# A recurrent attention block and a 64-expert feed-forward block on one core: three late shared tiles in place of four, a one-tile last batch, and the final wait on SyncE

## What is computed

```
x = x + attn(layernorm(x))       # r, k, v projections, a decayed running sum, a norm over the
                                 # whole sequence, an output projection
x = x + ffn(layernorm(x))
# ffn, E=64 experts of 512x384 (gate, up) and 384x512 (down), each token takes its best K=4:
logits = xf @ w_router.T ;  top_vals, top_idx = top_k(logits, 4) ;  w = softmax(top_vals)
per expert e, up to 64 tokens:  y = (silu(x_e @ w_gate[e]) * (x_e @ w_up[e])) @ w_down[e]
combined[token] += y * w
combined += (silu(xf @ w_sh_gate) * (xf @ w_sh_up)) @ w_sh_down     # shared expert, all 2048 tokens
```

## Time and profile before

| | us |
|---|---|
| median of 3 runs | 703.15 |
| lowest and highest | 702.74, 703.49 |
| span of the profiled execution, first to last instruction | 700.6 |
| PE busy | 666.0 (95%) |
| DVE busy | 324.1 (46%) |
| POOL busy | 218.7 (31%) |
| ACT busy | 162.1 (23%) |

### The profile page before, as it was taken

How to read it: one execution, slowest core, us unless ns; L and a number is a source line. 1 busy time by engine, 2 the same in 40 slices (tenths; PEclk the granted TensorE clock), 3 DMA queues, 4 the chain that set the end, 5 groups by cost and what they waited for, 6 DMA issues and landing times. The chain is left out here.

```text
span 700.6 us, 8995 instructions
## 1 busy us (share of the span) xinstructions
PE 666.0 (95%) x3229; PEld 402.0 (57%) x3229; DVE 324.1 (46%) x779; ACT 162.1 (23%) x267; POOL 218.7 (31%) x209
## 2 busy tenths in 40 slices
PE   4999999999999999999999999999999999999982
PEld 3687878888878754444455455455445554554430
DVE  6887567759868771332332233222323323232321
ACT  5922215633111411121211111111112112111210
POOL 5537446435648131022222102221221212212012
PEclk9999999999999999999999999999999999999997
DMA  8201006713784987599999999999999999999983
GB/s 321 77 27 35 1 31 201 265 60 123 269 313 192 354 307 271 210 376 387 388 405 404 385 369 389 399 391 404 370 387 388 402 372 384 387 403 395 362 322 43
DMA packets 52347, 202.65 MB, mean 289 GB/s; under 512 B 7340, under 2 KB 7468, under 8 KB 51920
## 3 DMA queue, kind: packets, MB, share of 16 engines
q1 hardware_dynamic: 36512, 169.23, 60.9%
q0 software_dynamic: 8928, 21.31, 12.7%
q10 hardware_dynamic: 6864, 11.54, 4.4%
HBM read 178.66 MB, written 23.59 MB: 289 GB/s over the span
## 5 line engine op out<-in xcount | busy, mean ns | idle before, releaser
L630 POOL DMA_INDIRECT out_dram<-ym,midx x32 | 51.3, 1602 | 297.1 <-DVE ym L1235 119.5
L1590 PE MATMUL bank<-w_sb,xT 128*64 128x384 f32 x768 | 129.1, 489 | 0.8 <-ACT xT L857 0.8
L1369 PE MATMUL bank<-x_hi,w_parts 128*128 128x512 f32 x368 | 115.0, 395 | 2.5 <-DVE x_lo L970 2.2
L1611 PE MATMUL bank<-w_sb,guT 128*64 128x512 f32 x384 | 88.0, 593 | 2.5 <-DMA w_sb<-in_L_ffn_w_down 2.0
L1590 PEld LDWEIGHTS bank<-w_sb,xT 128*64 128x64 f32 x768 | 53.0, 137 | 63.8 <-issue 60.1
L1369 PEld LDWEIGHTS bank<-x_hi,w_parts 128*128 128x128 f32 x368 | 69.7, 190 | 18.2 <-DVE x_lo L970 3.0
L1369 PE MATMUL bank<-x_lo,w_parts 128*128 128x512 f32 x184 | 71.0, 395 | 0.0
L1174 DVE TENSOR_TENSOR gu<-sg,bank 128x384 f32<-128x384 f32 x32 | 17.7, 554 | 114.3 <-issue 107.4
L1502 PE MATMUL bank<-sh_sb,xS 128*128 128x384 f32 x192 | 63.9, 486 | 0.0
L1611 PEld LDWEIGHTS bank<-w_sb,guT 128*64 128x64 f32 x384 | 27.6, 137 | 50.6 <-issue 50.5
L1502 PEld LDWEIGHTS bank<-sh_sb,xS 128*128 128x128 f32 x192 | 35.7, 191 | 22.3
(11 more groups left out here) (189 smaller groups left out, 949.3 us busy)
## 6 DMA issues: line engine op xcount, KB each, us to landing
w_sb<-in_L_ffn_w_down SPq DMA_DIRECT2D x64, 768.0 KB
w_sb<-in_L_ffn_w_gate SPq DMA_DIRECT2D x48, 768.0 KB, 19.2
w_sb<-in_L_ffn_w_up SPq DMA_DIRECT2D x48, 768.0 KB
extra<-in_L_ffn_w_gate SPq DMA_DIRECT2D x16, 768.0 KB
extra<-in_L_ffn_w_up SPq DMA_DIRECT2D x16, 768.0 KB
ring<-in_L_attn_x SPq DMA_DIRECT2D x14, 256.0 KB, 3.5
xt_dram<-xwT ACTq DMA_DIRECT2D x12, 256.0 KB, 2.8
xS<-xt_dram SPq DMA_DIRECT2D x12, 256.0 KB, 17.2
```

What stands on the lines that cost most here:

```text
L630: pool.indirect_dma_start(out=out[:, :], out_offset=bass.IndirectOffsetOnAxis(ap=midx[j % 3][u][:, :], axis=0), in_=ym[u][:, :], in_offset ...
L1369: ins = pe.matmul(ps[u][:, :], w, xp, start=(n == 0), stop=(n == len(parts) - 1))
L1590: ins = pe.matmul(ps[e * C:(e + 1) * C, 0:I], xT[:, c, e * C:(e + 1) * C], gate_up(2 * j + u, e, k)[:, c, :], start=(c == 0), stop=(c == K ...
L1611: ins = pe.matmul(pair_bank(j, u)[e * C:(e + 1) * C, :], guT[0][:, c, e * C:(e + 1) * C], down(2 * j + u, e)[:, c, :], start=(c == 0), sto ...
```

## The change

- `LEAD` goes from 4 to 3: tiles 13, 14 and 15 are late, and tile 12 becomes ordinary. Its residual and its transpose are now stored by ACT ahead of the groups, its transpose is read back by SP, and its result goes through `yS` and a batch.
- `FIRST` goes from 2 to 1: the 13 ordinary tiles are worked in groups 1 to 13. Group 0 has no shared tile of its own (it still finishes the third late one), nor have groups 14 and 15.
- The batches of three go out in groups 3, 6, 9 and 12, and one of one tile in group 13.
- SP no longer waits for `u_ready[2]` ahead of the up matrices of pair 3.
- The wait for the last add moves from the end of POOL's program to the end of SP's.

The places in memory that hang on `LATE` (the start of `extra`) move by one tile with it.

```diff
--- before.py
+++ after.py
@@ -51,11 +51,11 @@
 PIECES = 1
 FILL = 2 * PIECES * 16
 ADD = 16
-LEAD = 4
+LEAD = 3
 TAIL = 3
 SHARED = TOKENS // P - LEAD
 LATE = TOKENS // P - LEAD
-FIRST = 2
+FIRST = 1
 
 
 def moe_block(nc, x, wr, wk, wv, wo, decay, gn_w, gn_b, w_router, w_gate, w_up, w_down,
@@ -229,11 +229,11 @@
 
         def has_shared(j):
 
-            return j == 0 or FIRST <= j < FIRST + SHARED
+            return FIRST <= j < FIRST + SHARED
 
         def item(j):
 
-            return LEAD + j - FIRST if j else TAIL
+            return LEAD + j - FIRST
 
         def in_parts(j, u):
 
@@ -260,7 +260,11 @@
 
             return ap.rearrange("p (m c) -> p c m", c=n)[:, c, :]
 
-        BATCHES = range(FIRST + 2, FIRST + SHARED, 3)
+        BATCHES = [*range(FIRST + 2, FIRST + SHARED, 3), FIRST + SHARED - 1]
+
+        def batch(j):
+            last = j - FIRST
+            return last // 3 * 3, last + 1
 
         def landed(j, u):
 
@@ -469,7 +473,6 @@
                 sp.wait_ge(x2_stored[i], turned_stores(i))
                 sp.wait_ge(xw_stored[i], 16 * SEQS * TILES // 4)
             fill_matrix(sp, 3, 0)
-            sp.wait_ge(u_ready[2], 1)
             fill_matrix(sp, 3, 1, (1,))
             sp.wait_ge(tok_turned, 1)
             fill_matrix(sp, 3, 1, (0,))
@@ -482,6 +485,7 @@
                     load_matrix(p, k)
             load_down(2 * GROUPS - 2)
             load_down(2 * GROUPS - 1)
+            sp.wait_ge(added, landed(GROUPS - 1, 1))
 
 
         @block.gpsimd
@@ -640,8 +644,9 @@
                     pool.wait_ge(yS_ready, j - FIRST + 1 + LEAD)
                     pool.wait_ge(added, landed(j, 0))
                     pool.nop(nofuse=True)
-                    pool.dma_start(out[(j - FIRST - 2) * P:(j - FIRST + 1) * P, :].rearrange("(a p) m -> p a m", p=P),
-                                   yS[:, :, :], accum_op=ALU.add).then_inc(added, ADD)
+                    t0, t1 = batch(j)
+                    pool.dma_start(out[t0 * P:t1 * P, :].rearrange("(a p) m -> p a m", p=P),
+                                   yS[:, 0:t1 - t0, :], accum_op=ALU.add).then_inc(added, ADD)
                 add_pair(j, 1, landed(j - 1, 1) if j == GROUPS - 1 else landed(j, 0) + ADD * (j in BATCHES))
 
             for i in range(4):
@@ -662,7 +667,6 @@
                 if j == 0:
                     pool.wait_ge(late_stored, 16 * LEAD)
                 add_group(j)
-            pool.wait_ge(added, landed(GROUPS - 1, 1))
 
 
         @block.scalar
@@ -898,9 +902,7 @@
                     turned_tokens(j + 1, 0)
                 else:
                     pair_out(j, 1)
-                if first:
-                    store_late(TAIL)
-                elif shared:
+                if shared:
                     shared_out(j - FIRST)
 
             def shared_turn_copy(t):
@@ -1292,8 +1294,6 @@
                 else:
                     turn_copy(j, 1)
                 merged_out(j, 0)
-                if first:
-                    shared_residual(TAIL)
                 same_tokens(j, 1)
 
             for j in range(GROUPS):
@@ -1621,8 +1621,6 @@
                 turn_tokens(j, 1)
                 if first:
                     down_shared(TAIL - 1)
-                    for w in range(2):
-                        late_product(TAIL, w)
                 elif shared:
                     for w in range(2):
                         shared_product(j - FIRST, w)
```

## The result

| | before | changed |
|---|---|---|
| median of 20 runs, us | 702.75 | 704.67 |
| lowest and highest | 702.05, 703.53 | 701.48, 706.10 |
| ratio, 95% interval | | 1.0023 (1.0016 to 1.003) |
| profiled execution, its own time | not shown | 704.01 |
| its span | 700.6 | 702.2 |

The forecast was 699.6 us with a range of 696.8 to 703.4, and the median lies above the range. The two spans differ by 1.6 us, the medians by 1.9. The sum had a change of -3.5, so 5.1 us of the span have to be accounted for.

The account below looks back on a forecast made before the run. Groups bound by PE while weights arrive in time, otherwise by DMA; the end by the chain of adds and POOL's drain. -0.5 - 1.0 + 0.4 + 0.9 - 3.3 = -3.5 us from 703.15 gives 699.6 us, range 696.8 to 703.4.

Parts of the forecast that it names:

- Step 1: Shared tile moved from group 0 to group 1: group 2 starts at 311.40 against 311.87, -0.5 us.
- Step 2: Weights land 3.4 us sooner at the end, so an add there meets less traffic: -1.0 us (0 to -1.5).
- Step 3: Chain of adds to `out`, group 12 to group 13: 54.2 us against 53.8, +0.4 us (-3.7 to +1.6).
- the rival of the one-tile batch: Group 13's one-tile batch costs as much as three tiles, link 15.8 us instead of 9.4: 706.0 us; chance 0.05.
- Step 4: Ahead of the groups, SP's loads slide towards the first gather and delay it: +0.9 us (0 to 3.3).
- Step 5: Last wait moved to SP at the program's end, POOL's drain runs beside the last add's landing: -3.3 us (bound 0).
- the first rival: At the program's end, POOL's drain waits for the adds, 3.4 us from the landing on: 703.0 us; chance 0.12.
- the two rivals: At the end, POOL's drain waits for the adds, 703.0 us (0.12); ahead of the groups, gather delayed 3.3 us, 702.0 (0.09).
- The signs of being wrong: POOL's drain ending over 3 us after landing; group 13's second add over 2 us off 668 + 0.9; groups after 265 us.

Follow-up runs that it names:

- The filler: Changed kernel with three products that nobody reads added on PE ahead of its wait for the first gathered tokens; 702.71 us, ratio to before 0.9999.

## Why the prediction was wrong

- **Step 1** (-0.5): right, -0.48.
- **Step 2** (-1.0): the mechanism was right. PE's wait of 1.99 us on the weights is gone, and in its place PE waits as long for the adds, as the step said: L1611 at 679.98 us stands behind 1.86 us of waiting for DVE's copy to `ym`. The add issued at 679.95 takes 4.70 us where it took 6.00, 1.3 less. The net up to the last add is -0.4, since the last adds wait for DVE's copies and not only for the add before, inside the bounds of 0 to -1.5.
- **Step 3** (+0.4): right. From the first add of group 12 to the second of group 13 it is 670.67 - 616.57 = 54.1 us (forecast 54.2), and the one-tile link is 670.67 - 660.79 = 9.9 (forecast 9.4). The rule of the Trainium skill, "DMA: Bandwidth & Descriptors", section "Anatomy of one DMA", by which three tiles and one differ by 1.2 us, does not hold for these adds under full DMA, where the two differ by 5.6 us: the links take 9.9, 12.1 and 15.5 us for one, two and three tiles (the last 641.51 - 625.99). So the rival of the one-tile batch, the one that would have made it slower, was false.
- **Step 4** (+0.9): failed by its size, +2.9 measured. The gather's delay, for which the step had bounds of 0 to 3.3, was 1.2, near what I took. What the sum lacked was the second effect: a wait of 2 us makes the product behind it run at the lower clock, which costs 1.7 us more (7.07 against 5.38). The sum put it at nothing, without a word on it. The filler shows that this part comes with PE's idleness. The trace before could not price it at this place, but it had a wait of 0.8 us there, and any delay was going to lengthen just that wait. The delay of SP's load was read as "a few us"; it was 5.9, and the first 2.4 of such a delay cost nothing.
- **Step 5** (-3.3): failed, -0.7 in the trace, and 0.8 and 0.6 us by the medians of two pairs of runs, the second inside the spread. The step took POOL's drain for a fixed time that could run while the add was landing. Its other bound, 0, and the first rival (0.12) were nearly right: the drain waits for the landing. I had set against that rival that the drain took 3.4 us although all had landed. The run with work ahead of the drain shows that this spoke for neither: the time is paid even 5.6 us after the landing, and can't be paid before it. The section "The DRAIN you can't avoid" in the Trainium skill's "VectorE: DVE Perf Modes" gives its 12 ns for the drains that the runtime puts ahead of a kernel and behind it. The drains of this program's own end (L66) take 7 ns on SP after the change (123 ns before), but 705 on DVE, 717 on ACT and 3419 on POOL in the kernel before, so the figure is no price for them, though the time that I had worked out from it, with hardly any gain, was nearer than mine.

Step 5 misses by 2.6 us, step 4 by 2.0 and step 2 by 0.6, 5.2 together; steps 1 and 3 take 0.1 back, which makes the 5.1 to be explained. Either of the two large misses alone, put on the forecast, gives 702.2 or 701.6, inside the stated range; with step 4's cause undone the kernel runs in 701.33. It took both, and I had counted the two rivals as if only one could come. The signs of being wrong that the prediction named did not catch this well: the drain ended 3.0 us after the landing, just at its limit, and the other two limits were not reached (670.67 for the second add of group 13, 263.74 for the groups).

One reading ahead of the sum was also off, without an effect on it: the 2.6 us from the span to the median are not all outside the span. The changed kernel's profiled execution has 704.01 - 702.2 = 1.8 us outside it, and the rest is that execution's distance from the median.

## What to carry to other kernels

When a change adds a store that a later load waits for, read what that load shares the DMA engines with once it is late, and price the wait that it makes on TensorE twice: the wait, and the product behind it at the lower clock. A drain whose length is known only after everything has landed can't be assumed to overlap with the landing; only a run with the wait elsewhere tells. In a chain of adds, where the large batch stands counts, not only its size (moving it from group 12 to group 11 was worth 3.6 us here, while shrinking the last batch with the large one in group 12 gained nothing): keep it far enough from the end for the chain to catch up.

## What had not been expected of the hardware

- POOL's drain at the end of the program: 3419 and 3501 ns with the wait on POOL, 8.5 to 14.3 us when it is begun before the last add has landed; it ends 3.5 to 3.7 us after the landing in the first case and 2.9 to 3.0 in the second. Begun 5.6 us after the landing it still takes 3419 ns. SP's takes 7 ns in the same place.
- A wait of 1.97 us (with 0.72 us of work and 0.77 of waiting behind it) is followed by a granted clock of 0.50, while waits of 0.8 us in the same place leave it at 1.00. Three products that nobody reads, 2.1 us of PE's time, save 2.0 us of the changed kernel's.
